# Perceiver block on one core: head-attention row operations moved between phases, a wider zero product, and another order of loads at a stage seam

## The reference, cut to what matters

```python
x = x + cross_attention(layernorm(x), ctx, ctx, ...)   # x: 8 x 64 x 512, ctx: 8 x 1601 x 512, 16 heads of 32
x = x + encoder_layer(layernorm(x), ...)               # "head attention" and a feed-forward of 2048
x = x + moe_ffn(layernorm(x), ...)                     # 32 experts, 6 of them for each token

def head_attention(h):              # for each token alone: attention between its 2 x 16 heads
    q = split(h @ Wq.T) * 16 ** -0.5          # (token, 32, 16)
    k = split(h @ Wk.T)                       # (token, 32, 16)
    v = (h @ Wv.T)                            # (token, 16, 32)
    att = softmax(nan_to_num(q @ k.T))        # (token, 32, 32)
    att2 = att[:16, :16] - lam * att[16:, 16:]
    out = rmsnorm(att2 @ v) * (1 - LAMBDA_INIT)
    return out @ Wo.T + bo
```

## Time and profile before

| what | value |
|---|---|
| median of 3 runs | 1643.4 us (1642.81 to 1647.3) |
| the profiled execution: its own time | 1644.29 us |
| the profiled execution: span from the first to the last instruction | 1642.4 us |
| TensorE busy, mean granted clock | 90% of the span, 0.953 |
| DVE, ACT, POOL busy | 53%, 34%, 37% |

### The profile page before, as it was taken

The page is one execution under the profiler, slowest core; times in us unless marked ns, Lnnn a source line. Parts: engine busy times, 40 slices in busy tenths (PEclk is TensorE's granted clock), DMA queues, the critical chain, the costliest instruction groups (busy, mean ns, idle before and its releaser), DMA issues. The chain is left out here.

```text
span 1642.4 us, 23883 instructions
## 1 busy us (share of the span) xinstructions
PE 1475.2 (90%) x8888; PEld 1204.5 (73%) x8888; DVE 872.8 (53%) x2181; ACT 562.3 (34%) x1040; POOL 606.2 (37%) x287
## 2 busy tenths in 40 slices
PE   3399999999999999999999999489994749999994
PEld 3389999989898989898989898346663635555552
DVE  6144555455387655478655478548304634444442
ACT  4033443444443443443443443312122002232321
POOL 5501503303464803455803454336202223434442
PEclk9699999999999999999999999799996869999997
DMA  3500102112101112102012100720002079999999
GB/s 113 188 7 26 63 7 62 59 39 89 51 7 61 34 65 93 53 8 61 34 65 93 53 1 1 282 103 1 1 1 110 1 283 333 333 337 341 330 343 293
DMA packets 58064, 181.68 MB, mean 111 GB/s; under 512 B 6130, under 2 KB 23026, under 8 KB 47860
## 3 DMA queue, kind: packets, MB, share of 16 engines
q1 hardware_dynamic: 47796, 156.28, 26.3%
q0 software_dynamic: 10176, 24.12, 5.9%
HBM read 158.36 MB, written 22.02 MB: 110 GB/s over the span
## 5 line engine op out<-in xcount | busy, mean ns | idle before, releaser
L65 PE MATMUL ps_x<-wkv_hi,c_hi 128*128 128x256 f32 (+1 forms) x832 | 241.6, 290 | 0.0
L67 PE MATMUL ps_x<-wkv_hi,c_lo 128*128 128x256 f32 (+1 forms) x832 | 234.8, 282 | 0.0
L66 PE MATMUL ps_x<-wkv_lo,c_hi 128*128 128x256 f32 (+1 forms) x832 | 234.7, 282 | 0.0
L65 PE MATMUL ps_x<-c_hi,wkv_hi 128*128 128x402 f32 x512 | 196.0, 383 | 35.8 <-POOL c_lo L415 35.8
L412 POOL TENSOR_TENSOR c_hi<-c_raw,ones 128x1608 fp32r<-128x1608 f32 x32 | 91.8, 2870 | 346.2 <-DMA c_raw<-ctxT 346.2
L841 DVE TENSOR_TENSOR pT<-ps_x,pT 128x512 fp32r<-128x512 f32 (+1 forms) x224 | 145.1, 648 | 135.3 <-ACT pT L711 132.7
L711 ACT CAST pT<-ps_x 128x512 fp32r<-128x512 f32 (+1 forms) x224 | 124.6, 557 | 180.7 <-PE ps_x L581 177.6
L67 PE MATMUL ps_x<-c_hi,wkv_lo 128*128 128x402 f32 x512 | 178.0, 348 | 0.0
L66 PE MATMUL ps_x<-c_lo,wkv_hi 128*128 128x402 f32 x512 | 177.8, 347 | 0.0
L65 PEld LDWEIGHTS ps_x<-wkv_hi,c_hi 128*128 128x128 f32 (+1 forms) x832 | 154.1, 185 | 17.1 <-issue 17.1
L692 ACT CAST vv<-ps_x 128x512 fp32r<-128x512 f32 (+1 forms) x112 | 62.1, 554 | 281.4 <-PE ps_x L67 281.4
(11 more groups left out here) (328 smaller groups left out, 2776.5 us busy)
## 6 DMA issues: line engine op xcount, KB each, us to landing
e_w_gu<-w_gu SPq DMA_DIRECT2D x49, 1024.0 KB, 8.4
c_raw<-ctxT SPq DMA_DIRECT2D x32, 804.0 KB, 5.0
e_w_dn<-w_dn SPq DMA_DIRECT2D x48, 512.0 KB, 5.9
x_tok<-slabs SPq DMA_DIRECT2D x13, 1024.0 KB, 4.9
spare<-slabs SPq DMA_DIRECT2D x8, 1024.0 KB, 8.1
qbd_dram<-qbd_all SPq DMA_DIRECT2D x2, 2048.0 KB, 6.9
qbd<-qbd_dram SPq DMA_DIRECT2D x16, 256.0 KB, 4.8
h_late<-slabs SPq DMA_DIRECT2D x4, 1024.0 KB, 15.7
```

The costliest lines, as they stand in the source:

```text
L65: nc.tensor.matmul(out, a_hi, b_hi, start=start, stop=False)
L66: nc.tensor.matmul(out, a_hi, b_lo, start=False, stop=False)
L67: return nc.tensor.matmul(out, a_lo, b_hi, start=False, stop=stop)
```

## The change: what it does

1. `behind_values` and `behind_turn`: the 16 first reductions of a tile stand behind all seven value steps of h = 0 (before: five of them) and behind turns 0 to 8 (before: 0 to 10), `clean_low` and `clean_high` behind turns 9 and 10 (before 11 and 12), and `row_max` in the next unit's first value step (before: behind turn 13). In h = 1 `less_max` goes from value step 0 to 1, the exponential from 1 to 2, `row_sum` from 2 to 3. Of the last eight reductions four (before: five) stand in h = 1 of b = 3 and 5, and the other four in the value phase of the next batch. In the last unit two stand in the value phase and six behind turns 1, 2, 4, 6, 8 and 9 (before: four and four, the last behind turn 6), `mean_square` and `root` three turns later, and ACT's root behind turn 12 (before 9).
2. The zero product is made from all 128 rows of `zero` (before: 32).
3. The row of biases for cross attention lies in `att` and is loaded anew for each tile; before it was loaded once, to row 32 of its own buffer.
4. At the seam SP sends first the three rows, the tile of x, `x1_in` and `on_in`, then slabs 1 and 2, waits for the last reduction, and sends slab 0 and slabs 4, 3, 5, 6, 7, 8.
5. Tile 2's head output `on` stays in SBUF and is no more stored and loaded again. `onT` has three buffers; `turn_o(2)` is made right behind `turn_o(0)` and `turn_o(1)`, and ACT copies all three at once.

```diff
@@ cross_attention, SP @@
             def load_x(t):
                 if t:
                     sp.wait_ge(x1_stored, 16 * t)
+                    sp.wait_ge(w01_done, 2 * t)
                 sp.dma_start(x1[:], a["x"][P * t:P * t + P]).then_inc(xt_loaded, 16)
+                sp.dma_start(row, a["rows"][0:1]).then_inc(row_loaded, 16)
...
             sp.wait_ge(v_full, B * 14)
-            for s in (1, 2, 3, 4):
-                sp.dma_start(keep["slabs"][s], a["slabs"][s]).then_inc(keep["w_loaded"][s], 16)
+            for r, line in enumerate(keep["rows"]):
+                if r == 0:
+                    sp.wait_ge(w01_done, 2 * (TT - 1))
+                sp.dma_start(line, a["rows"][r:r + 1]).then_inc(keep["row_loaded"], 16)
             sp.wait_ge(x1_stored, 16 * (TT - 1))
             sp.dma_start(x1[:], a["x"][P * (TT - 1):]).then_inc(keep["x_loaded"], 16)
+            sp.dma_start(keep["x1_in"], a["x1_dram"].rearrange("(t p) d -> p t d", p=P)).then_inc(keep["tiles_loaded"], 16)
+            sp.wait_ge(on_stored, 16 * (TT - 2))
+            sp.dma_start(keep["on_in"], a["on_dram"].rearrange("(t p) d -> p t d", p=P)).then_inc(keep["tiles_loaded"], 16)
+            for s in (1, 2):
+                sp.dma_start(keep["slabs"][s], a["slabs"][s]).then_inc(keep["w_loaded"][s], 16)
             sp.wait_ge(red_done, 24 * (TT - 1))
-            sp.dma_start(slab[:], a["slabs"][0].rearrange("p k n -> p (k n)")).then_inc(keep["w_loaded"][0], 16)
-            store_on(TT - 2)
-            for s in (5, 6):
-                sp.dma_start(keep["slabs"][s], a["slabs"][s]).then_inc(keep["w_loaded"][s], 16)
-            sp.dma_start(keep["x1_in"], a["x1_dram"].rearrange("(t p) d -> p t d", p=P)).then_inc(keep["tiles_loaded"], 16)
-            sp.wait_ge(on_stored, 16 * (TT - 1))
-            sp.dma_start(keep["on_in"], a["on_dram"].rearrange("(t p) d -> p t d", p=P)).then_inc(keep["tiles_loaded"], 16)
-            for s in (7, 8):
-                sp.dma_start(keep["slabs"][s], a["slabs"][s]).then_inc(keep["w_loaded"][s], 16)
+            for s in (0, 4, 3, 5, 6, 7, 8):
+                place = slab[:].rearrange("p (k n) -> p k n", k=KD) if s == 0 else keep["slabs"][s]
+                sp.dma_start(place, a["slabs"][s]).then_inc(keep["w_loaded"][s], 16)
@@ cross_attention, TensorE @@
-                    nc.tensor.matmul(ps[:, 4 + g], zero[0:32, 0:P], zero[0:32, :], start=True, stop=False)
+                    nc.tensor.matmul(ps[:, 4 + g], zero[:, 0:P], zero[:], start=True, stop=False)
...
-                nc.tensor.matmul(ps[:, AUX], ones[32:33, :], row[32:33, :], start=True, stop=False)
+                nc.tensor.matmul(ps[:, AUX], ones[0:1, :], row, start=True, stop=False)
@@ cross_attention, ACT @@
-                    if v == 1 and h == 1 and old is not None:
+                    if v == 2 and h == 1 and old is not None:
                         head_exponentials(old)
...
-                        if last and (g, t) == (1, 2):
+                        if last and (g, t) == (1, 5):
                             root(TT - 2)
@@ cross_attention, DVE @@
             def behind_values(b, h, v):
                 t = tile_in(b)
-                if t and h == 0 and v < 3:
-                    reduce(t - 1, 21 + v)
+                if t and h == 0 and v < 4:
+                    reduce(t - 1, 20 + v)
...
-                if h == 0 and v in (0, 1, 3, 4, 6):
-                    reduce(t, (0, 1, None, 2, 3, None, 4)[v])
-                if h == 1:
-                    if v == 0:
-                        less_max(t)
-                    if v == 2:
-                        row_sum(t)
-                    if b == B - 1 and v in (4, 5, 6):
-                        reduce(t, 12 + v)
-                    if b == B - 1 and v == 6:
-                        reduce(t, 19)
+                if h == 0:
+                    reduce(t, v)
+                    return
+                if v == 0:
+                    row_max(t)
+                if v == 1:
+                    less_max(t)
+                if v == 3:
+                    row_sum(t)
+                if b == B - 1 and v > 4:
+                    reduce(t, 11 + v)
...
                 if h == 0:
-                    if n < 11:
-                        reduce(t, 5 + n)
+                    if n < 9:
+                        reduce(t, 7 + n)
+                    if n == 9:
+                        clean_low(t)
+                    if n == 10:
+                        clean_high(t)
+                elif b < B - 1:
+                    if n in (8, 9, 10, 12):
+                        reduce(t, 16 + (0, 1, 2, None, 3)[n - 8])
+                else:
+                    if n in (1, 2, 4, 6, 8, 9):
+                        reduce(t, 18 + (1, 2, 4, 6, 8, 9).index(n))
                     if n == 11:
-                        clean_low(t)
-                    if n == 12:
-                        clean_high(t)
+                        mean_square(t)
                     if n == 13:
-                        row_max(t)
-                elif b < B - 1:
-                    if n in (8, 9, 10, 12, 13):
-                        reduce(t, 16 + (0, 1, 2, None, 3, 4)[n - 8])
-                else:
-                    if n in (1, 3, 4, 6):
-                        reduce(t, 20 + (None, 0, None, 1, 2, None, 3)[n])
-                    if n == 8:
-                        mean_square(t)
-                    if n == 10:
                         root(t)
@@ last_head_and_feed_forward @@
-        onT = sb("h_onT", [P, 2, KD, P])
+        onT = sb("h_onT", [P, 3, KD, P])
...
-            sp.dma_start(row[:], a["rows"].rearrange("(o r) d -> o r d", o=1)).then_inc(row_loaded, 16)
...
-            turned_o(0)
+            for t in range(HT):
+                turned_o(t)
...
             query_key(1)
-            turned_o(1)
...
             turned_c(0)
-            turned_o(2)
...
             turn_o(1)
+            turn_o(2)
             put_out(0)
...
             put_out(1)
-            turn_o(2)
             turn_c(0)
             put_out(2)
```

More of the change, by code:

```diff
@@ L294, in cross_attention @@
         AUX = 3
-        row = nc.alloc_sbuf_tensor_at("t_row", [P, D], F32, offset=nc.sbuf_base - 4 * D)
+        row = att[0:1, 0:D]
         def tile_in(b):
@@ L383, in _ @@
                     load_queries(c, c)
-            sp.wait_ge(zero_done, 1)
-            sp.dma_start(row[32:33, :], a["rows"][0:1]).then_inc(row_loaded, 16)
             sp.dma_start(small["lam4"][:], a["lambdas"].partition_broadcast(P)).then_inc(small_loaded, 16)
@@ L1042, in unit @@
                         behind_turn(b, h, g, t)
-            nc.vector.memset(f32(zero[:]), 0.0).then_inc(zero_done, 1)
+            nc.vector.memset(f32(zero[:]), 0.0)
             for j in range(2):
@@ L1115, in last_head_and_feed_forward @@
         late = sb("h_late", [P, 4, KD, D])
-        row = sb("h_row", [1, 3, D])
+        row, row_loaded = keep["rows"], keep["row_loaded"]
         cols2, b1 = sb("h_cols2", [P, 2, KD]), sb("h_b1", [P, FT])
@@ L1137, in last_head_and_feed_forward @@
         z1 = vprod[:, 0]
-        row_loaded, c_loaded = sem("h_row_loaded"), sem("h_c_loaded")
+        c_loaded = sem("h_c_loaded")
         o_biased, x1_full, x1_done = sem("h_o_biased"), sem("h_x1_full"), sem("h_x1_done")
@@ L1236, in turned_o @@
                 act.wait_ge(onT_full, t + 1)
-                if t >= 2:
-                    act.wait_ge(src_full, t - 1)
-                nc.scalar.copy(onT[:, t % 2], ps[:, ON_BANK[t]].rearrange("p (k n) -> p k n", k=KD)).then_inc(onT_done, 1)
+                if t == 3:
+                    act.wait_ge(src_full, 1)
+                nc.scalar.copy(onT[:, t % 3], ps[:, ON_BANK[t]].rearrange("p (k n) -> p k n", k=KD)).then_inc(onT_done, 1)
             def query_key(w):
@@ L1427, in turn_o @@
             def turn_o(t):
-                if t < HT:
+                if t < 2:
                     pe.wait_ge(tiles_loaded, 32)
-                else:
+                if t == 3:
                     pe.wait_ge(on_done, 1)
-                if t == 2:
-                    pe.wait_ge(onT_done, 1)
-                if t == 3:
                     pe.wait_ge(cT_done, 1)
-                src = on_in[:, t] if t < HT else on
+                src = on_in[:, t] if t < 2 else on
                 for g in range(KD):
@@ L1449, in put_out @@
                     pe.wait_ge(hT_done, 1)
-                nc.tensor.matmul(ps[:, OUT_BANK[t]], ones[0:1, :], row[0:1, 1], start=True, stop=False)
+                nc.tensor.matmul(ps[:, OUT_BANK[t]], ones[0:1, :], row[1], start=True, stop=False)
                 for g in range(KD):
-                    ins = nc.tensor.matmul(ps[:, OUT_BANK[t]], onT[:, t % 2, g], weight(W_OUT)[:, g], start=False, stop=(g == KD - 1))
+                    ins = nc.tensor.matmul(ps[:, OUT_BANK[t]], onT[:, t % 3, g], weight(W_OUT)[:, g], start=False, stop=(g == KD - 1))
                 ins.then_inc(src_full, 1)
@@ L1456, in project @@
```

(18 more changed lines are left out.)

6 lines of the change are left out of this document (3 added, 3 removed).

## The result

Four executions of the changed kernel took 1617.36 to 1620.58 us, median 1619.63; four of the kernel before, 1642.81 to 1647.3, median 1644.26 (the 1643.4 that I started from is the median without the profiled one). The ratio is 0.9846, with an interval of 0.9827 to 0.9864. The time lies 1.1 us above the forecast and inside its narrower range, 1614 to 1623.

The account below looks back on a forecast made before the run. TensorE was taken as the bound, apart from the seam's DMA wait and DVE-paced odd units. Terms -10.1 - 10.5 - 4.4 - 1.4 + 1.2 + 0.3 = -24.9 us took median 1643.4 to 1618.5 us; range 1612 to 1630, narrower 1614 to 1623.

Parts of the forecast that it names:

- seam: Between cross attention and the next stage: L1505 starts at 1058.4 instead of 1068.54 with rows sent first, -10.1 us.
- zero product: Start of units: using all 128 rows saves 0.39 us at each of 27 products, -10.5 us.
- row order, up to the last unit: DVE's reductions moved: odd units' gaps -4.4, clock dip -1.4, wait before the last unit's turn 0 -1.2 us.
- last unit's turns: Last unit of cross attention: six reductions behind the turns instead of four, +2.4 us.
- third tile early: Tile 2's transpose ahead of put_out(0): +0.3 us; the feed-forward's 2.5 us earlier start is lost waiting at turn_c(2).
- gaps: TensorE's waits at the two last turns of b = 3, 5, 7's first halves go: 3 x 1.48, -4.4 us.
- dip: Lower granted clock after the gaps in the first odd unit goes with them, -1.4 us.
- slack for slab 0: At the seam: slab of W_O lands at 1054, leaving 4 us before TensorE's start at 1058.35.
- My first rival: Zero product's cost is not in its rows, so widening gives 0: 1629.0 us, chance 0.20.
- The second rival: DVE stays the pace of the odd units, gaps and dip remain: 1624.3 us, chance 0.14.
- The slower rival: Value phase has no room; reductions hold up score copies, over 8.3 us per odd batch: 1644 us, chance 0.02.
- that cover: Value phase hides the two added reductions in odd first halves; without it 2 x 1.21 a unit, 7.3 us in all.

Follow-up runs that it names:

- rows sent last: Changed kernel with the three rows of biases sent behind slabs 0, 4, 3 and 5 to 8: 1628.77 us, ratio 0.9907.
- the second profile: Changed kernel as it is, run once more with five executions on one chip: 1617.29 us, ratio 0.9831.
- 128 rows alone: Kernel before with only the zero product over all 128 rows, the row of biases moved to make room: 1635.41 us, ratio 0.9948.
- 32 rows again: Changed kernel with the zero product put back to 32 rows: 1628.82 us, ratio 0.9900.
- third tile late: Changed kernel with tile 2's transpose, ACT copy and waits put back to their places before, still from SBUF: 1615.66 us, ratio 0.9831.
- the one with fillers: Changed kernel with turn_c(2) and ACT's exponential later, plus unread products in the last unit's turns and at the seam: 1611.13 us, ratio 0.9800.
- the filled seam: Changed kernel with five unread zero products behind the last selection and eight transposes at the next stage's start: 1618.92 us, ratio 0.9828.

## Why the prediction was right, term by term

| term | forecast | measured | by |
|---|---|---|---|
| seam | -10.1 | -10.16 | both traces; rows sent last +10.6 |
| clock behind the seam | 0 | +1.3, in this execution; 0.0 in the second profile | windows |
| zero product | -10.5 | -10.5 alone | 128 rows alone |
| row order, up to the last unit | -7.0 | -6.9 alone | 32 rows again |
| the two together | 0 | -1.0 more | both traces, 18.45 in all |
| last unit's turns | +2.4 | -0.2; +0.8 on average | both traces; all profiles |
| third tile early | +0.3 | 0 | third tile late |
| clock behind `turn_c(2)` | 0 | +1.4, in this execution | windows |
| routing and experts | 0 | +3.0 | both traces, no edit there |

(My -7.0 is the gaps' 4.4, the dip's 1.4 and the 1.2 less of waiting before the last unit's turn 0, which I had booked under the last unit. Alone the order gives 911.69 - 904.76 = 6.9 from first to last zero product.) The remaining 19.14 - 18.45 = 0.69 us lie ahead of the first zero product.

**Seam: right.** The slack for slab 0 held, the gap is POOL's, and with the rows sent last the old wait returns.

**Zero product: right.** 0.39 us each, as read from the earlier trace rows, and 27 of them in the kernel before: with all rows alone, 10.5 us. Beside the new order it is 11.5: an odd batch's first half then gains 0.5 to 0.6 us from its two products and not 0.25 to 0.4, since DVE no longer sets the pace there, and the unit behind it gains 0.9 and not 0.8. I had costed the two parts as if they did not meet, and that is the 1.0 us. My first rival falls. The Trainium skill (TensorE: Matmul & The Clock Gate, section Why this matters for your kernels) says that a single product on 32 rows takes as long as one on 128. No run here has such a product by itself; carried over to one that stands between products on all rows, the rule fails, by 1.28 against 0.89 us for the stretch.

**Row order: right.** Waits and dip are gone. The second rival, DVE remaining the pace, would have left waits of 0.7 us at the last turns; there are none. The slower rival's mechanism does exist, at an eighteenth of what it needed: the key product at 709.73 waits 0.20 us for the last score copy, and the unit is 0.46 us longer, three times, where 8.3 were wanted. I had called that cover free. The odd first half pays it back: with 32 rows it takes 57.66 us and not 59.66, 2.0 less where I had 1.48.

**Last unit: the term was mis-sized.** I charged two more reductions behind the turns in full (+2.4). The averages over all profiles are 22.4 us with the old order and 23.2 with the new one, so they cost 0.8, and in this execution nothing. DVE has room between the turns: these go at 1.6 us each by a chain through ACT and DVE. Most of the spread from 22.2 to 24.0 goes with the clock: the three executions of 22.2 to 22.6 us have a mean granted clock of 0.91 to 0.92 over the turns, the seven of 23.3 to 24.0 have 0.85 to 0.87, and the one with fillers has 1.00 and 21.59 us. The old order's three lie between, at 0.88 to 0.89. Drawn through these at an equal clock, my estimate of what the two reductions cost is 0.6 us. The 1.2 us less of waiting before turn 0 (4.18 to 3.05) did arrive.

**Third tile: right.** The wait at `turn_c(2)` was to grow to 4.8 us; it is 3.39, with 1.21 at `turn_c(1)`, 4.6 in all. I took the transpose for +0.3; 53.25 against 53.31 us says 0. What I had not seen is that a wait of that length can cost the clock.

That the error is only 1.1 us is partly luck, since it is smaller than what it is made of. Against the forecast the traces have -0.7 ahead of the first zero product, -1.0 up to the last, -2.6 in the last turns and -0.1 at the seam, and on the other side +1.3 and +1.1 with the clock behind it and +3.0 in routing and experts. The second profile of the changed kernel, with a span of 1615.5 us, is 27.0 us shorter than the one before, where I had said 24.9: its start is 2.0 us shorter, the clock behind the seam and at `turn_c(2)` costs no more than in the kernel before, and the experts have the same +2.7.

## What to carry to other kernels

Put small loads that the next stage's first instruction needs ahead of the large ones on the same queue, and read the name behind the arrow at the seam. Before counting a saving, find the next place where the engine waits for something else: the third tile's 2.5 us were gone at `turn_c(2)`, and moving that one step by three, with ACT's exponential by four, was worth 3.6 us in the stretch. Where one part takes an engine's waits away, count the other part's savings as if they were already gone.

## What the runs showed of the hardware that I had not expected

- A product on 32 or on 64 rows between products on 128 costs 0.39 us more than one on all 128 in the stretch around it, 1.28 us against 0.89: its weight load and the next one do not run beside the product ahead.
- The clock can fall without a long gap: in the filled seam it fell at 1033.7, where TensorE was busy 0.95 of 2 us, then 0.58 and 0.66 of 1 us. With fillers in the last unit it stayed full.
- The same wait can cost the clock or not. Behind 3.36 to 3.40 us at `turn_c(2)` it fell in 2 of 7 profiled executions, for 1.4 and 2.7 us. With the old order it fell behind two waits of 0.75 us in one of the three odd units: in b = 3 of the kernel before, in b = 5 of both runs that kept this order.
- The experts' stretch takes 316.7 to 317.5 us in five of the fourteen profiled executions and 319.4 to 321.8 in the other nine, with the same code. The kernel before fell among the short, the changed one among the long: 2.7 us of the difference between the two traces. The difference arises at one place, where TensorE is slower for lack of clock. These are the windows from 26 to 34 us behind the mark, before and after:

```profile
1351.00:1359.00 8.00, 5.02 (x18) 2.53 (x17) 2.92 (x14) 1.24 (x3) 1.80 (x2) 0.92 1.06 354
1324.50:1332.50 8.00, 5.02 (x12) 2.41 (x11) 1.99 (x8) 0.38 (x1) 1.37 (x1) 0.71 1.05 355
```

  The clock there is 0.91 to 0.93 in all five short ones and 0.71 in all nine long ones, and between the two traces TensorE falls behind by 2.4 us at this place and by next to nothing after it. What picks the one or the other stays open. The three profiles with the old row order are all short, against two of the eleven with the new one; I can't rule out that the order has a part in it.
